# One table of places for every piece of work: a hybrid block of attention, routed low-rank layer and state-space layer on one core

## What is computed

```python
def attn(x):                       # x is layernorm(x)
    xn = x * rsqrt(mean(x * x) + EPS) * norm_w
    q, k, v = heads(xn @ Wq.T + bq), heads(xn @ Wk.T + bk), heads(xn @ Wv.T + bv)
    p = softmax(where(causal, -inf, q @ k.T / 4))
    return xn + (p @ v) @ Wo.T + bo

def ffn(x):
    gate = softmax(x @ router_W.T + router_b)      # two largest of 6, renormalised
    h = x @ routed_A
    return x @ base_W.T + base_b + (x @ shared_A.T) @ shared_B.T + sum(w_e * (h_e @ routed_B_e.T))

def ssm(x):
    xc = silu(causal_conv4(x) + conv_b)
    delta = softplus(xc @ Wd.T + bd);  Bm = xc @ Wb.T;  Cm = xc @ Wc.T
    # for each state n: h = exp(A_n * dt) * h + dt * xc * B_n;  y += h * C_n
    return (y * sigmoid(x @ Wg.T + bg)) @ Wo.T + bo

x = x + attn(ln(x)); x = x + ffn(ln(x)); x = x + ssm(ln(x)); x = x + ffn(ln(x))
```

## Time and profile before

| | |
|---|---|
| median of 3 runs | 2170.35 us (2165.85 to 2177.23) |
| span of the profiled execution | 2159.4 us, 33647 instructions |
| mean granted TensorE clock | 0.956 |
| PE, DVE, ACT, POOL busy | 85%, 78%, 65%, 48% of the span |
| DMA | 275.53 MB, mean 128 GB/s |

### The profile page before, as it was taken

The page is one execution under the profiler, slowest core; times in us unless marked ns, Lnnn a source line. Parts: engine busy times, 40 slices in busy tenths (PEclk is TensorE's granted clock), DMA queues, the critical chain, the costliest instruction groups (busy, mean ns, idle before and its releaser), DMA issues.

```text
span 2159.4 us, 33647 instructions
## 1 busy us (share of the span) xinstructions
PE 1842.8 (85%) x11409; PEld 1132.2 (52%) x11440; DVE 1684.1 (78%) x2586; ACT 1407.4 (65%) x2724; POOL 1040.1 (48%) x930
## 2 busy tenths in 40 slices
PE   5779888998989798988989898898989898877775
PEld 3446454645556464645556464655656464635333
DVE  5343678889788888879787888879887888987783
ACT  2445767686676767677675867677675767574531
POOL 0000364556555464646555464646555464666430
PEclk8999999999999999999999999999999999999998
DMA  4312377666767576667767686666767676652110
GB/s 115 83 52 59 93 152 153 145 142 150 159 140 159 124 170 140 151 128 154 158 148 157 129 171 130 146 142 149 156 141 157 133 157 135 139 112 61 45 59 10
DMA packets 185916, 275.53 MB, mean 128 GB/s; under 512 B 33537, under 2 KB 125586, under 8 KB 185746
## 3 DMA queue, kind: packets, MB, share of 16 engines
q1 hardware_dynamic: 155506, 163.27, 30.5%
q0 software_dynamic: 30240, 110.11, 27.6%
HBM read 128.58 MB, written 34.08 MB: 75 GB/s over the span
## 4 chain that ended last, share of the span: by engine, by line
PE 44%; ACT 19%; DMA 16%; SPq 7%; issue 6%; DVE 5%; POOL 2%; ACTq 0%; POOLq 0%; DVEq 0%
PE bank L314 7%; DMA sk<-qk_parts 7%; PE bank L518 5%; PE bank L323 5%; SPq L726 5%; ACT dec L910 3%; PE bank L372 3%; ACT pt L795 3%; PE bank L395 3%; PE bank L420 3%; PE bank L501 3%; DMA qk_parts<-parts 3%; DMA out<-X 3%; PE bank L482 3%; PE bank L308 2%
## 5 line engine op out<-in xcount | busy, mean ns | idle before, releaser
L1158 DVE TENSOR_TENSOR_SCAN hc<-dec,inp 128x1024 f32<-128x1024 f32 x256 | 613.1, 2395 | 33.0 <-ACT dec L910 28.6
L1331 POOL TENSOR_TENSOR inp<-u,b_all 128x512 f32<-128x512 f32 x256 | 341.1, 1332 | 421.9 <-DVE hc L1158 177.5
L795 ACT ACTIVATE pt<-bank 128x512 f32<-128x512 f32 x640 | 373.8, 597 | 220.4 <-PE bank L397 217.6
L372 PE MATMUL bank<-sk,sq 96*128 96x512 bf16 (+3 forms) x1024 | 279.6, 312 | 95.4 <-DMA sk<-qk_parts 64.4
L1337 POOL TENSOR_TENSOR inp<-u,b_all 128x512 f32<-128x512 f32 x240 | 350.0, 1458 | 18.8
L910 ACT ACTIVATE dec<-dt,a_neg 128x511 f32<-128x511 f32 x512 | 338.0, 717 | 31.4 <-DVE hc L1158 31.4
L1167 DVE TENSOR_TENSOR hc<-hc,bank 128x1024 f32<-128x1024 f32 x242 | 293.6, 1213 | 50.6 <-PE bank L557 49.9
L395 PE MATMUL bank<-sq,sk 98*128 98x512 bf16 (+3 forms) x1024 | 275.4, 307 | 34.1 <-ACT pt L795 28.1
L1344 POOL DMA_DIRECT2D y<-hc x210 | 185.6, 884 | 244.8 <-DMA y<-hc 122.9
L1026 DVE TENSOR_REDUCE mall<-bank 128x1 f32<-128x512 f32 x256 | 172.6, 674 | 100.3 <-PE bank L374 100.0
L372 PEld LDWEIGHTS bank<-sk,sq 96*128 96x128 bf16 x1024 | 102.3, 100 | 213.9 <-DMA sk<-qk_parts 73.0
(11 more groups left out here) (168 smaller groups left out, 3534.2 us busy)
## 6 DMA issues: line engine op xcount, KB each, us to landing
y<-hc POOLq DMA_DIRECT2D x210, 512.0 KB, 5.5
b_all<-b_kept SPq DMA_DIRECT2D x256, 256.0 KB, 4.0
qk_parts<-parts SPq DMA_DIRECT2D x96, 256.0 KB, 2.5
sq<-qk_parts SPq DMA_DIRECT2D x384, 64.0 KB, 3.6
sk<-qk_parts SPq DMA_DIRECT2D x384, 64.0 KB, 3.8
X<-in_x SPq DMA_DIRECT2D x16, 512.0 KB, 5.9
out<-X SPq DMA_DIRECT2D x16, 512.0 KB, 5.9
sq<-hlt SPq DMA_DIRECT2D x256, 2.0 KB
```

The source lines that it names most:

```text
L372: mm(dst[:, o:o + n], sq[0:KS, slot, h, qb * P:(qb + 1) * P], sk[0:KS, slot, h, 0:n], start=True, stop=False)
L795: A(pt[:, n % PT, :], score_bank[unit % 2][:, :], ACT.Exp).then_inc(exp_done.sem, 1)
L1158: V.tensor_tensor_scan(h, d, v, 0.0, ALU.mult, ALU.add).then_inc(scan_done.sem, 1)
L1331: first = G.tensor_tensor(inp[:, n % 2, 0, :], u[:, 0, :], b_all[:, k % 3, :], ALU.mult)
```

## The change

All places now come from the tables PE_AT, BANK, ACT_AT, DVE_AT, POOL_AT and SP_AT: scans, products, decays, inputs, additions and B loads have one position for each of the 16 states, and the pieces of a group have theirs. The loops over units and positions become one loop over positions in each queue. New helpers: `group(now, at)` tells which group is due, `steps(now, at)` which states. Nearly every number of the tables is new. B's rows pass through the first half of `tok_f`, the buffer of the normalised tokens, instead of `hwt`, with the waits moved to match. `project_v` of the first batch waits for the constants, and the statistics of a batch wait for the normalisation of the one before. Instructions, shapes and transfers are otherwise the same. The diff, cut to its core:

```diff
     KS = len(TERMS) * HD
     NT = 2 * len(TERMS)
     NQ = NG * NB
 
-    STEP_AT = {0: 0, 2: 1, 5: 2, 7: 3}
-    PRODUCT_AT = {1: 0, 3: 1, 6: 2, 8: 3}
-    DECAY_AT = {1: -1, 4: 0, 5: 1, 8: 2}
     LATE = NB - 2
     FIRST, END = -6, NQ + 12
 
 
-    FRAME = 2 * UN * NG
-    PE_AT = {"res": (-32, -31), "xn": (-75, -71), "qk00": (-52, -50, -48), "qk01": (-50, -47, -44), "v": (-26, -32),
-             "qk10": (-6, -4, -3), "qk11": (-4, -2, 0), "ao": (92, 92), "x1": (95, 97), "turn0": (105, 108),
-             "low0": 109, "hw0": 121, "up0": (124, 125), "xs": (135, 135), "conv": (137, 141), "gate": (146, 140),
-             "bc": (149, 152, 154), "dt": (149, 152), "x3": (251, 252), "turn1": (262, 265), "low1": 265, "hw1": 275,
-             "up1": (278, 279)}
-    BANK = {"res": (0, 1), "xn": (1, 0), "qk00": 0, "qk01": 1, "v": (0, 1), "qk10": 0, "qk11": 1, "ao": (0, 1),
-            "x1": (1, 1), "turn0": (1, 1), "low0": 1, "hw0": 1, "up0": (0, 1), "xs": (1, 0), "conv": (1, 1),
-            "gate": (1, 0), "bc": 1, "dt": (0, 0), "x3": (0, 1), "turn1": (0, 1), "low1": 0, "hw1": 0, "up1": (1, 0)}
-    ACT_AT = {"res": (-30, -28), "square_f": 98, "square_s": 127, "square_l": 252, "norm_q": -94, "norm_f": 103,
-              "exp0": 115, "norm_s": 131, "softplus": 153, "decays": 160, "norm_l": 257, "exp1": 266,
-              "xn": (-76, -71), "qk00": (-52, -50, -47), "qk01": (-50, -49, -44), "v": (-26, -32),
-              "qk10": (-6, -4, -1), "qk11": (-4, -2, 0), "ao": (91, 92), "turn0": (104, 108), "low0": 110,
-              "hw0": 120, "xs": (135, 138), "conv": (139, 141), "gate": (146, 140), "bc": (149, 152, 154),
-              "dt": (149, 152), "turn1": (263, 263), "low1": 264, "hw1": 275}
-    DVE_AT = {"add_x1": (94, 96), "in0": 113, "out0": 116, "add_up0": (123, 124), "silu": 144, "delta": 155,
-              "gated": 246, "add_x3": (251, 251), "in1": 265, "out1": 268, "add_up1": (277, 280), "stats_q": -102}
-    POOL_AT = {"rsqrt_f": 99, "rsqrt_s": 124, "rsqrt_q": -104, "inputs": 151, "rsqrt_l": 254, "low": (111, 266)}
-    SP_AT = {"parts": (-43, -4), "load_x": -119, "store_b": 155, "store": 281}
-    FINISH = 14
-    HEADS_PE, HEADS_DVE = 4, 4
-
+    HALF = 2 * UN
+    FRAME = HALF * NG
+    START, STOP = HALF * FIRST, HALF * END
+    PE_AT = {"res": (-31, -29), "xn": (-75, -70), "qk00": (-57, -48, -46), "qk01": (-47, -45, -44),
+             "qk10": (-6, -2, -1), "qk11": (-4, -2, 0), "v": (-29, -32), "ao": (88, 91), "x1": (91, 94),
+             "turn0": (108, 110), "low0": 112, "hw0": 123, "up0": (126, 127), "xs": (137, 137), "conv": (139, 140),
+             "gate": (142, 142), "bc": (149, 151, 156), "dt": (145, 150), "x3": (248, 251), "turn1": (258, 260),
+             "low1": 264, "hw1": 276, "up1": (277, 278), "values": (10, 18, 21), "heads": 26,
+             "b": (158, 160, 164, 168, 171, 174, 186, 190, 195, 200, 206, 208, 213, 218, 224, 234),
+             "c": (157, 169, 171, 175, 180, 185, 194, 196, 200, 207, 210, 217, 219, 224, 230, 235),
+             "sum": (167, 175, 181, 184, 187, 193, 198, 204, 208, 210, 215, 220, 230, 236, 240, 241)}
+    BANK = {"res": (1, 0), "xn": (1, 0), "qk00": 0, "qk01": 1, "v": (1, 0), "qk10": 0, "qk11": 1, "ao": (0, 1),
+            "x1": (0, 1), "turn0": (1, 1), "low0": 1, "hw0": 1, "up0": (0, 1), "xs": (0, 1), "conv": (0, 1),
+            "gate": (0, 1), "bc": 1, "dt": (0, 0), "x3": (1, 0), "turn1": (0, 1), "low1": 1, "hw1": 0, "up1": (0, 1)}
+    ACT_AT = {"res": (-30, -29), "square_f": 100, "square_s": 127, "square_l": 252, "norm_f": 103, "norm_s": 130,
+              "norm_q": -105, "norm_l": 253, "exp0": 116, "exp1": 269, "softplus": 150, "xn": (-77, -73),
+              "qk00": (-50, -47, -46), "qk01": (-47, -46, -44), "qk10": (-5, -2, -1), "qk11": (-4, -2, 0),
+              "v": (-27, -30), "ao": (85, 91), "turn0": (107, 110), "turn1": (258, 260), "xs": (135, 136),
+              "low0": 111, "low1": 266, "hw0": 121, "hw1": 276, "conv": (138, 139), "gate": (142, 146),
+              "bc": (148, 152, 153), "dt": (146, 150), "heads": 20,
+              "decays": (154, 162, 163, 170, 172, 176, 188, 191, 196, 196, 209, 214, 215, 218, 224, 227)}
+    DVE_AT = {"gated": 245, "add_x3": (249, 250), "in0": 113, "in1": 266, "out0": 116, "out1": 271,
+              "add_up1": (278, 278), "add_x1": (94, 94), "add_up0": (125, 127), "silu": 141, "delta": 153,
+              "stats_q": -111, "finish": -9, "heads": 27,
+              "scan": (156, 168, 168, 171, 180, 184, 191, 193, 203, 208, 209, 216, 217, 218, 226, 232),
+              "product": (156, 169, 171, 176, 183, 190, 192, 196, 205, 208, 212, 216, 217, 222, 230, 233)}
+    POOL_AT = {"rsqrt_f": 93, "rsqrt_s": 129, "rsqrt_q": -110, "rsqrt_l": 247, "low": (111, 259),
+               "inputs": (150, 155, 156, 161, 169, 172, 176, 176, 192, 202, 206, 211, 214, 218, 222, 225),
+               "add": (160, 161, 169, 175, 177, 189, 189, 194, 206, 209, 212, 214, 221, 222, 229, 232)}
+    SP_AT = {"parts": (-42, -1), "load_x": -114, "store_b": 149, "store": 278, "stack": (-31, -31, -31),
+             "maxima": -5, "load_b": (149, 154, 154, 156, 168, 170, 177, 181, 189, 194, 196, 206, 208, 213, 218, 226)}
     ctx = ExitStack()
     with ctx:
         def sb(name, shape, dt=F32):
@@ -205,7 +210,7 @@
         wts = sb("wts", [P, 2, TB, E + 1])
         hw = sb("hw", [P, 2, TB, ER + 1])
         hwt = sb("hwt", [ER + 1, T])
-        b_rows = hwt[0:NS, :]
+        b_rows = tok_f[0:NS, 0:2, :].rearrange("p t d -> p (t d)")
         xs_t = sb("xs_t", [P, C, TAPS - 1 + T])
         xc = sb("xc", [P, C, T])
...
+
+        def group(now, at):
+
+            g, rest = divmod(now - at, HALF)
+            return g if rest == 0 and 0 <= g < NQ else -1
+
+        def steps(now, at):
+
+            return [(a, n) for n in range(NS) if (a := due(now, at[n])) >= 0]
 
 
         w_first = sem("first_weights_loaded")
...
                 m = side["v", j]
+                if a == 0:
+                    pe.wait_ge(dve_const, 1)
                 for c in range(C):
                     pe.wait_ge(side["xn", c].free, side["xn", c].at("xn", a, c))
...
-                if q == -2:
+            for now in range(START, STOP):
+                if now == -2 * HALF:
                     pe.wait_ge(dve_const, 1)
-                for p in range(UN):
-                    if 0 <= UN * q + p + LM < UN * NQ:
-                        max_unit(UN * q + p + LM)
-                    side_work(2 * (UN * q + p))
-                    if 0 <= q < NQ:
-                        score_unit(q, p)
-                    if p in PRODUCT_AT:
-                        spread_b(k + PRODUCT_AT[p] + 1)
-                        spread_c(k + PRODUCT_AT[p])
-                        sum_y(k + PRODUCT_AT[p] - 1)
-                    if 0 <= q - 1 < NQ:
-                        if p == 0:
-                            values_b(q - 1)
-                        elif p == 1:
-                            values_c(q - 1)
-                        if p == HEADS_PE:
-                            turn_heads(q - 1)
-                    if p == 7 and 0 <= q < NQ:
-                        values_a(q)
-                    side_work(2 * (UN * q + p) + 1)
+                unit, odd = divmod(now, 2)
+                if not odd and 0 <= unit + LM < UN * NQ:
+                    max_unit(unit + LM)
+                side_work(now)
+                if not odd and 0 <= unit < UN * NQ:
+                    score_unit(*divmod(unit, UN))
+                for a, n in steps(now, PE_AT["b"]):
+                    spread_b(a, n)
+                for a, n in steps(now, PE_AT["c"]):
+                    spread_c(a, n)
+                for a, n in steps(now, PE_AT["sum"]):
+                    sum_y(a, n)
+                if (g := group(now, PE_AT["values"][1])) >= 0:
+                    values_b(g)
+                if (g := group(now, PE_AT["values"][2])) >= 0:
+                    values_c(g)
+                if (g := group(now, PE_AT["heads"])) >= 0:
+                    turn_heads(g)
+                if (g := group(now, PE_AT["values"][0])) >= 0:
+                    values_a(g)
 
 
         @block.sync
...
             for dst, src in rest:
                 sp.dma_start(dst, src).then_inc(w_rest, 16)
-            for q in range(FIRST, END):
-                k = NG * q - LK
-                for p in range(UN):
-                    if p < 3 and 0 <= q + 2 < NQ:
-                        stack(q + 2, p)
-                    if p in STEP_AT and (k + STEP_AT[p]) % NS < NS - 3:
-                        load_b(k + STEP_AT[p] + 3)
-                    for now in (2 * (UN * q + p), 2 * (UN * q + p) + 1):
-                        for j in range(2):
-                            if (a := due(now, SP_AT["parts"][j])) >= 0:
-                                store_parts(a, j)
-                        if (a := due(now, SP_AT["store"])) >= 0:
-                            store(a)
```

(47 more changed lines are left out.)

162 lines of the change are left out of this document (65 added, 97 removed).

## The result

| | before | after |
|---|---|---|
| median of the runs | 2168.1 us (4 runs, 2165.06 to 2177.23) | 2034.26 us (4 runs, 2025.73 to 2037.55) |
| span of the profiled execution | 2159.4 us | 2023.9 us |
| PE, DVE, ACT, POOL busy | 85%, 78%, 65%, 48% | 90%, 84%, 70%, 55% |

The ratio is 0.9382, with a 95% interval of 0.9349 to 0.9416. The kernel became 134 us faster.

What follows compares the result with a forecast made beforehand. Bound: TensorE's work plus about 13 us of standing still per 122.24 us period. Savings of 31.7 (parts) + 45.9 (banks) - 16.2 (bursts) = 61.4 us take 2170.35 to 2109 us; range 2065 to 2172 us.

Steps and rivals of the forecast that it cites:

- The code and B's buffer: Copying B's rows through another buffer, with four moved or new waits, was to do nothing by itself: 0 us.
- The stacked parts' waits: TensorE's 42.3 us of waits for stacked query and key parts should go; three quarters taken, 31.7 us saved.
- The bank waits: TensorE's waits around side banks MA and MB, at projections, low-rank product and weighted rows' turn: 45.9 us net saved.
- the two new ones: New waits of 1.0 us a period each at the first matmuls of x1 and qk11, charged within the bank terms.
- (c): VectorE becomes the bound as maxima queue behind bursts of scans: 2216 us at the charge's upper bound; chance 0.08.
- (b): ScalarE and GpSimd queues stopping early give the gain back in small waits, 4.7 us a period: 2170 us; chance 0.10.
- Rival (a): Whole saving: bursts free, all parts' waits gone, half the exp and maxima waits gone: 2062 us; chance 0.22.
- (d): SBUF port: five scans a period lose 1.27 us each to GpSimd's reads, none hidden: 2193 us; chance 0.05.
- Burst charge: Late maxima behind two bursts of VectorE scans and products a period, 0.62 us each: 16.2 us lost.
- Start and end: Before 300 us and after 1900 us, same work and order matters little: 0, bounds 20 us either way.
- The last quarter of the parts' waits: Share of the stacked-parts waits left out of the saving because the margin was small and queues shared: 10.6 us.
- TensorE's work, 108.8 us a period: TensorE's busy time per period was to stay near 109 us, as no matmul changes; a change would void the sum.

Runs made afterwards that it cites:

- tables_before: The changed code with the old positions and banks written into its tables, keeping the new buffer of B's rows: 2163.5 us, ratio 0.9998.
- after_side_by_scan: The changed kernel with the first burst's second scan at 163, its product at 166, C's row at 165, decays unmoved: 2100.67 us, ratio 0.9712.
- before_new_side: Old positions, but new places and banks of all stages and group pieces, with GpSimd's small stages left old: 2467.96 us, ratio 1.1434.
- before_new_dma: Old positions in the changed code, but new DMA-queue places for parts' stores and loads, load_x and store: 2201.65 us, ratio 1.0171.
- before_new_steps: Old positions, but new places for the states' steps (scans, products, inputs, decays, spreads, B loads): 2585.25 us, ratio 1.1974.
- after_old_dma: The changed kernel with the old DMA-queue places of parts' stores and loads, load_x and store: 2055.84 us, ratio 0.9502.
- after_no_pool_reads: The changed kernel with GpSimd's two products of inputs replaced by constant fills that read nothing: 2004.23 us, ratio 0.9291.
- the mixtures: Kernels combining old stages, banks and group pieces with new state steps, or the reverse, with old or new DMA places: four runs, 2466.16 to 2585.25 us.

## Why the prediction was right and wrong

**Right.** The bound: TensorE's work plus its pauses, with VectorE close behind. The code and B's buffer: nothing (tables_before). The stacked parts' waits in after: 1.6 us in eleven periods, where I had said "below 15 us". The bank waits went one by one, and the two new ones of about 1 us came at the two places named, 1.4 and 0.9 us. TensorE's wait for maxima stayed small, so (c) is out. The time rules out (b) for after, but its sign showed: the waits for exps grew from 14.8 to 23.8 us in eleven periods, behind a softplus that I hadn't looked at. Rival (a) was the nearest in time, and its waits for exps and maxima, of which half was to go, grew instead from 31.6 to 37.2 us. The rule of the Trainium skill in (d) ("SBUF — State Buffer", Who interferes with whom) holds more fully than the row on which I sized it. My row showed a third of GpSimd's time lost; in after both lose:

```profile
862.21 3.63 DVE L1151 TENSOR_TENSOR_SCAN hc<-dec,inp 128x1024 f32<-128x1024 f32 x1 [0.20 <-ACT dec L915]
```
```profile
862.11 1.57 POOL L1320 TENSOR_TENSOR inp<-u,b_all 128x512 f32<-128x512 f32 x1
863.76 3.15 POOL L1326 TENSOR_TENSOR inp<-u,b_all 128x512 f32<-128x512 f32 x1
```

The scan of 2.29 us took 3.63 and GpSimd's product of 1.27 us took 3.15. What failed in (d) was its last step, that none of it hides: with these reads the time is 2034 us and not 2193, and without them the period is the same.

**The terms that failed.** Two terms were put at nothing, the start and TensorE's work, and the charge for bursts had the wrong sign. Each in turn.

**Burst charge, 16.2 us.** In after the waits for maxima fell from 16.8 to 13.4 us in eleven periods. I had noted that the bursts stand beside TensorE's full stretches, and charged for them all the same. The reverse side was missing: work of VectorE in a thin stretch lets TensorE outrun it. What bursts save by themselves is not shown, since the one run on it (after_side_by_scan, 66 us slower) also met late decays.

**Start and end, 0 within 20 us.** The end held (1.3 us). The start gave 35.1 us, 23.8 of them before the first convolution. No scan runs there. The softplus of batch 0 comes at 231.4 us in before, at 205.9 in before_new_side, at 225.3 in before_new_dma and at 231.0 in before_new_steps. So the stages' places are worth some 26 us there and the DMA places, alone, some 6; beside the new stages they add next to nothing (204.3 us in after, 205.1 in after_old_dma). I had said that latency rules there and drew "the order matters little"; in a chain of stages with nothing beside it a place counts in full.

**The last quarter of the parts' waits** went as well, about 10 us, as in rival (a).

**TensorE's work, 108.8 us a period, taken as constant.** It fell to 106.3, which is 27.5 us. Part of this is the clock. The clock records have TensorE at 1.2 GHz for 64.8 us of before's eleven periods and for 41.0 us of after's, and half of the difference, some 12 us, is my estimate for its share. The other 15 us or so are open. By groups of matmuls: projections of the state output (L337, `wso,y`) went from a mean of 425 ns to 379, while those behind the new pause at qk11 (L328, `xt_q,wqk`) went from 602 to 708. The windows around that pause in after, with the granted clock in the third column from the right:

```profile
890.00:893.70 3.70, 1.42 (x8) 0.60 (x8) 3.67 (x4) 3.58 (x7) 1.26 (x1) 0.94 0.90 223
893.70:897.20 3.50, 3.47 (x7) 1.52 (x8) 2.66 (x3) 2.31 (x4) 3.40 (x4) 0.57 0.26 70
```

TensorE was busy for 1.42 of 3.70 us, and the next 3.5 us ran at 0.57, close to the lower level of 1.2 GHz. So a removed wait can pay more than its length. The sum of the pauses doesn't tell how much: after_no_pool_reads has less of them than after and more time at 1.2 GHz. I had named this as what would void the sum, and gave it no term.

**Together.** The forecast's terms were for 13.1 periods. Scaled to eleven they are 26.6 us for the parts, 38.5 for the banks and 13.6 against for the bursts, 51.6 in all. Measured in the eleven periods:

| | forecast | measured |
|---|---|---|
| stacked parts (39.8 to 1.6) | 26.6 | 38.2 |
| banks (62.6 gone, 26.9 new) | 38.5 | 35.7 |
| maxima (16.8 to 13.4) | -13.6 | 3.4 |
| exps (14.8 to 23.8) | 0 | -9.0 |
| other waits of TensorE | 0 | 3.3 |
| TensorE's work | 0 | 27.5 |
| eleven periods | 51.6 | 99.1 |

The start (35.1) and the end (1.3) make it 135.5 us.

**The step beneath them all** was to price each table's distances by themselves and add. As a reading of after's waits it came out nearly right; as a statement on what each part does it was false: alone, the DMA places cost 37 us, the stages 300 and the steps 420. Rival (b), queues that stop early give it back, comes nearest to what the mixtures do, and I priced it at 4.7 us a period; a single misplaced number measured 12.

**Open.** What holds the period at 113 us. It stayed between 112.8 and 114.0 us with the two bank waits gone, the softplus moved, both, or GpSimd's reads gone. VectorE's work by itself is not it: without the reads it is 99.7 us a period for 104.2 in after, and the period is the same. TensorE is busy for 106.3 us of it in after and for 107.8 there, and how its pauses and its clock go together was not taken apart. Also open is most of the loss in the mixtures: of 545 us, four numbers account for some 206.
